# Moving the head of the last layer ahead by one iteration, and weighing two key tiles per run, in a four-layer attention kernel

## The chip, the cores and the metric

One of the eight cores of a Trainium2 chip runs the kernel. The metric is the device time of one execution in microseconds (us), as the median of several runs.

## The reference

The input is a batch of 8 images of 256 channels and 32 x 32 points (1024 tokens each). Four attention layers follow one another; each image passes them alone, so the batches are independent.

```
layer 0: th, ph, g = three 1x1 convolutions to 32 channels; lat = softmax(th^T ph) g^T
         x = x + gamma_sa * conv(lat); then attention to 128 fixed concepts; x = x + gamma_moca * conv(lat2)
layer 1: q, k of 32 channels, v of 256; x = x + gamma * (softmax(q^T k) v)
layer 2: group norm; q, k, v of 256 channels, one head; x = x + proj(softmax(q^T k / 16) v)
layer 3: group norm; 8 heads of 32 channels; softmax attention; output projection wo;
         layer norm over the channels; x = x + the result
```

Every softmax is over 1024 keys for 1024 queries. Everything is in fp32 to the accuracy of the reference; the scores are formed from high and low parts in fp32r.

## The kernel before

**Two lanes.** The work of a batch b is two generators per engine: `front(b)` (layers 0, 1, 2) and `back(b)` (layer 3). Each yields after every small group of instructions. `batches` strings them together: first `front(0)` beside `front(1)`, then for b = 0 to 5 `front(b + 2)` beside `back(b)` (the main loop, six iterations), at last `back(6)` beside `back(7)`. `merged` takes from the one or the other by the table `ORDER`, written out by hand for each stage and engine: lengths of alternate stretches, beginning with the second lane. Within an engine the order is thus fixed, and an instruction that waits holds all behind it. The front lane owns four of the eight PSUM banks, the back lane the other four.

**A softmax layer.** PE forms the scores of one tile of 128 queries against all 1024 keys (`max_tile`, L627: two matmuls into two banks); DVE reduces them to a negated maximum per query (`maximum`, L1285). The maxima are turned into a row and multiplied in with the queries (`shift_rows`: on PE, L634, in the front lane; in the back lane by DVE's transpose and four small transfers of SP, L463). Then PE forms the scores again with keys on the partitions (`stacked_scores`, L641; in layer 2 L837 and L840), ACT takes the exp from PSUM (L1008 in the front, L1138 in the back), and PE weighs the values with them (L697, L755, L918). The sums of the weights come from adds on POOL (L523, L555) and DVE (L1446) and a matmul with ones (L762, L930); ACT inverts them by Ln and Exp (L1017, L1020), DVE multiplies (L1334, L1454).

**The back lane.** Its head: group norm (DVE L1348 and small steps, PE L797 and L801, ACT L1054 to L1060, result in `hb`), queries and keys of the first four heads (PE L608, ACT casts the high parts L1067, DVE the low parts L1280, into `part`), the values (PE L616, copies to `vb` L1025 and L1326). SP then copies `part` into the stacks `qs` and `ks` of the four heads with 24 transfers (L477, 128 KB each). Then two rounds u = 0, 1 of four heads each (`both_rounds`): `maxima(u)`, 4 x 8 tiles; `middle(u)`, in round 0 the queries and keys of the other four heads; `steps(u)`, 16 steps, one for each tile of 128 keys and half of the queries. A step has four score matmuls (one per head) into three banks taken in turn; `score_use` and `total_use` number their uses, `bank_use` tells whose exp frees a bank. The four exps of a step go to `prb`, which holds two steps. `weigh(s - 1)`, issued between the second and third scores of step s, is four matmuls with 32 columns each, side by side in column tiles of the array (L918; eight instructions, as an fp32 matmul is two). Last come the output projection (L608), the layer norm (L958, L1187 to L1206, L1498, L1502) and the store; when a back is through, SP loads the image for its buffer (L488).

**Stages of an iteration in the rows.** A, 754.6 to 863.5 us: the front's layer 0 beside the back's head, its first maxima and the second projections. B, to 953.2: layer 1 beside the first 16 steps. C, to 1007.2: the group norm and projections of layer 2 beside the second maxima. D, to 1119.8: attention of layer 2 beside the second 16 steps, the output projection and the layer norm.

## Time and profile before

| what | value |
|---|---|
| median of 3 runs | 3000.66 us (2998.16 to 3001.39) |
| the profiled execution | 3000.55 us, span 2998.4 us |
| mean granted clock of TensorE | 0.89 |
| PE matmul / weight load busy | 91% / 47% |
| DVE, ACT, POOL busy | 60%, 40%, 30% |
| fronts stage ends, first iteration ends | 392.7 us, 754.6 us |
| the iteration shown below | 754.6 to 1119.8 us, 365.2 us |
| last stage begins | 2577.3 us |

A busy time sums the durations of an engine's instructions without overlap. A matmul at half clock is busy twice as long, so a high busy share does not say that PE is at its peak. "Idle before" gives the time the engine stood before the instruction and what it is inferred to have waited for.

### The profile page before, as it was taken

The numbers are of one execution on the slowest core, as the hardware profiler recorded it, in microseconds if no ns is written. First come the engines' busy times: TensorE is split into PE (matmuls) and PEld (weight loads), VectorE is DVE, ScalarE is ACT, GpSimd is POOL, SyncE is SP. The second block draws the span as 40 slices with busy tenths as digits, with TensorE's granted clock in tenths as the row PEclk, the third lists the DMA queues.
The fourth block names the chain that finished last, engine by engine and source line by source line (L and its number), as shares of the span: only waits on it lengthen the run. The fifth ranks groups of instructions, "written<-read, shape, count | busy, mean of one in ns | idle before, by whom it ended". The sixth has DMA issues, their size and how long they took to land.

```text
span 2998.4 us, 25561 instructions
## 1 busy us (share of the span) xinstructions
PE 2740.4 (91%) x9636; PEld 1415.0 (47%) x9636; DVE 1795.9 (60%) x1749; ACT 1209.4 (40%) x2073; POOL 897.0 (30%) x362
## 2 busy tenths in 40 slices
PE   7999989999899998999889998999989989798887
PEld 4546644455444544445444454444544445443332
DVE  4535057673676647765476654767447583488884
ACT  3332223535344442534426254262532625325455
POOL 0040311614025240333304242061510615115563
PEclk8899988989788998989979898798987989879787
DMA  2000010100201002010010100101020100211100
GB/s 83 1 0 0 1 43 1 43 1 6 65 1 43 1 17 54 1 42 1 28 43 1 42 1 29 42 14 30 1 56 15 40 3 1 64 36 43 43 1 28
DMA packets 29291, 72.08 MB, mean 24 GB/s; under 512 B 10224, under 2 KB 10416, under 8 KB 28912
## 3 DMA queue, kind: packets, MB, share of 16 engines
q1 hardware_dynamic: 29168, 70.45, 9.4%
q8 instruction: 76, 1.25, 0.2%
q14 instruction: 47, 0.39, 0.0%
HBM read 11.40 MB, written 8.39 MB: 7 GB/s over the span
## 4 chain that ended last, share of the span: by engine, by line
PE 71%; DVE 17%; issue 3%; ACT 3%; SPq 2%; DMA 2%; POOL 1%; DVEq 0%; ACTq 0%; POOLq 0%
PE ps L755 13%; PE ps L608 12%; PE ps L641 9%; PE ps L627 9%; PE ps L918 7%; PE ps L840 6%; DVE ba_nmx L1285 5%; PE ps L616 4%; SPq L477 2%; PE ps L697 2%; DVE accb L1446 2%; PE ps L826 2%; DVE fa_nmx L1285 1%; PE ps L930 1%; PE ps L837 1%
## 5 line engine op out<-in xcount | busy, mean ns | idle before, releaser
L1138 ACT ACTIVATE prb<-ps 128x512 f32<-128x512 f32 x896 | 489.1, 598 | 367.7 <-PE ps L641 341.1
L1285 DVE TENSOR_REDUCE ba_nmx<-ps 128x1 f32<-128x1024 f32 x448 | 531.0, 1215 | 77.9 <-PE ps L627 76.2
L555 POOL TENSOR_TENSOR accb<-accb,prb 128x1024 f32<-128x1024 f32 x168 | 440.8, 2624 | 179.0 <-ACT prb L1138 174.8
L627 PE MATMUL ps<-ks,qs 96*128 96x512 f32 x896 | 419.5, 575 | 74.6 <-DVE ba_nmx L1285 69.0
L555 POOL TENSOR_TENSOR accb<-prb 128x1024 f32<-128x1024 f32 x28 | 80.2, 2864 | 1306.8 <-ACT prb L1138 1247.3
L755 PE MATMUL ps<-pr,h 128*128 128x512 f32 x896 | 421.1, 594 | 0.2
L1446 DVE TENSOR_TENSOR accb<-accb,prb 128x1024 f32<-128x1024 f32 x168 | 317.8, 1892 | 155.8 <-ACT prb L1138 154.1
L641 PE MATMUL ps<-qs,ks 97*128 97x512 f32 x896 | 351.6, 464 | 8.6 <-ACT prb L1138 7.5
L627 PEld LDWEIGHTS ps<-ks,qs 96*128 96x128 f32 x896 | 195.3, 248 | 268.6 <-DVE ba_nmx L1285 201.9
L641 PEld LDWEIGHTS ps<-qs,ks 97*128 97x128 f32 x896 | 160.7, 192 | 228.1 <-ACT prb L1138 157.0
L1008 ACT ACTIVATE pr<-ps 128x512 f32<-128x512 f32 x336 | 194.5, 598 | 175.9 <-PE ps L641 112.5
L755 PEld LDWEIGHTS ps<-pr,h 128*128 128x128 f32 x896 | 167.4, 189 | 162.8 <-issue 143.4
L918 PE MATMUL ps<-prb,vb 128*32 128x512 f32 x1792 | 243.4, 616 | 0.7 <-ACT prb L1138 0.7
L1334 DVE TENSOR_TENSOR tmp<-tmp,rden 128x512 f32<-128x512 f32 x56 | 46.7, 866 | 311.9 <-ACT rden L1020 311.9
L1285 DVE TENSOR_REDUCE fa_nmx<-ps 128x1 f32<-128x1024 f32 x168 | 198.9, 1216 | 17.9 <-PE ps L826 12.2
L523 POOL TENSOR_TENSOR acc<-acc,pr 128x1024 f32<-128x1024 f32 x56 | 153.0, 2732 | 138.8 <-ACT pr L1008 138.8
L608 PE MATMUL ps<-hb,w 128*128 128x512 f32 x368 | 175.8, 632 | 2.0 <-ACT hb L1060 2.0
L840 PE MATMUL ps<-q2k 128*128 128x512 f32 x672 | 173.4, 393 | 0.0
L523 POOL TENSOR_TENSOR acc<-pr 128x1024 f32<-128x1024 f32 x28 | 69.1, 2467 | 338.8 <-ACT pr L1008 301.8
L840 PEld LDWEIGHTS ps<-q2k 128*128 128x128 f32 x672 | 126.7, 189 | 36.4 <-issue 10.3
L608 PE MATMUL ps<-h,w 128*128 128x512 f32 x272 | 139.1, 649 | 1.3 <-DVE bb_nmx L1285 1.3
L627 PE MATMUL ps<-ks,q2k 96*128 96x512 f32 x224 | 90.5, 509 | 36.2 <-DVE fa_nmx L1285 24.6
(303 smaller groups left out, 3402.4 us busy)
## 6 DMA issues: line engine op xcount, KB each, us to landing
qs<-part SPq DMA_DIRECT2D x168, 128.0 KB, 2.4
ks<-part SPq DMA_DIRECT2D x168, 128.0 KB, 2.4
xm<-in_x SPq DMA_DIRECT2D x8, 1024.0 KB, 5.6
out<-prb SPq DMA_DIRECT2D x28, 256.0 KB, 2.0
q2k<-part SPq DMA_DIRECT2D x48, 128.0 KB, 2.4
w<-in_weights SPq DMA_DIRECT2D x1, 2592.0 KB, 8.7
out<-pr SPq DMA_DIRECT2D x4, 256.0 KB, 2.0
qs<-ba_nmx_r SPq DMA_DIRECT2D x56, 4.0 KB, 1.8
```

What stands on the lines that cost most here:

```text
L523: pool.tensor_tensor(o.acc[:], before if jg == 1 else o.acc[:], now, ALU.add).then_inc(o.summed[n].sem, 1)
L555: pool.tensor_tensor(o.sums[1], o.pairs[(s - 1) % 2][1] if j == 1 else o.sums[1], o.pairs[s % 2][1], ALU.add)\
L608: mm = pe.matmul(o.ps[0:m, bank, :], wcol(name, kt, m0, m), src[:, kt, cols(ic)], start=kt == 0, stop=kt == CH - 1)
L627: mm = pe.matmul(o.ps[:, bank + jc, :], queries[0:STACK, tile(it)], keys[0:STACK, cols(jc)], start=True, stop=True)
L641: return pe.matmul(o.ps[:, bank, :], keys[0:ROW + 1, tile(jt)], queries[0:ROW + 1, cols(ic)], start=True, stop=True)
L755: mm = pe.matmul(o.ps[:, 2 + ch, :], o.v[:, jt, tile(ch)], o.pr[:, t % 4, :], start=jt == 0, stop=jt == NT - 1)
L840: mm = pe.matmul(o.ps[:, bank, :], kpart[:, kt, keys], qpart[:, kt, cols(ic)], start=False, stop=kt == CH - 1 and kpart is o.kl2)
L918: mm = pe.matmul(o.ps[L * g:L * g + L, 2, :], o.vb[:, jt, L * (QUAD * u + g):L * (QUAD * u + g + 1)], weights3(o, s, g), start=jt == 0, st ...
L1008: act.activation(o.pr[:, t % 4, :], o.ps[:, bank, :], ACT.Exp).then_inc(o.exped[n].sem, 1)
L1138: act.activation(weights3(o, s, g), o.ps[:, turn3[score_use(s, g) % 3], :], ACT.Exp)\
L1285: dve.tensor_reduce(o.nmx[:, head, it:it + 1], o.ps[:, bank:bank + 2, :], AX.XY, ALU.max, negate=True).then_inc(o.max_sb[n].sem, 1)
L1446: dve.tensor_tensor(o.sums[0], o.pairs[(s - 1) % 2][0] if j == 1 else o.sums[0], o.pairs[s % 2][0], ALU.add)\
```

## The change

It does two things. **The head.** `back(b)` now yields the word "head" when its head is issued (on PE after the values, on ACT and DVE after the copies of the values, on SP after the first stacks, on POOL at once). `batches` makes the backs beforehand and appends the head of `back(b + 1)` behind `back(b)` on its lane, beside the front of the same iteration; the head of `back(0)` is appended behind `front(1)`, whose buffers it takes over. The lane then begins the next iteration with the first maxima. **Two tiles of keys.** For batches 0 to 5 (`in_pairs`) PE weighs at even steps only, after the first two scores: `weigh(s - 2)` and `weigh(s - 1)` one behind the other, 16 column-tiled instructions; the last pair follows the last scores. For batches 6 and 7 it stays one per step. The first sum of weights takes its bank two uses later and ACT's inversion moves by two exps, in all batches.

The tables `ORDER` are all new. What stands in them for the main loop, on PE, read off by counting:

| | before | after |
|---|---|---|
| head: norm, q, k, v | among the front's first 13 items | norm after score 13 and 14 of layer 2, q and k after score 15; v behind the front's last item |
| first maxima (32) | 2 before the front's scores of layer 0, 15 more beside these and the weighing, rest to the end of layer 0 | 8 before them, 7 of them beside the 8 front tiles; 9 beside the scores, rest to the end of layer 0 |
| second projections | before the front's last four matmuls of layer 0 | behind them |
| second maxima (32) | 8 before the sum that ends layer 1, 24 behind it | all behind it, the last two beside the first tiles of layer 2's maxima |
| second 16 steps | begin before layer 2's maxima | begin before the last of the 8 tiles |
| output projection | near layer 2's score 14 | near its score 11 |

On DVE the reductions are placed alike: before, 23 back tiles lie between the front's last maximum and its first transpose of layer 0, after the change 14. In the fronts stage the head comes behind the last item of both fronts. In the last stage `back(6)` begins with maxima, beside the head of `back(7)`.

The diff without the tables:

```diff
@@ -147,12 +149,21 @@
         pass
 
 
+def head(last_layer):
+
+    for slot in last_layer:
+        yield
+        if slot == "head":
+            return
+
+
 def batches(engine, front, back):
 
-    finish(merged("fronts", engine, front(0), front(1)))
+    last = [back(b) for b in range(B)]
+    finish(merged("fronts", engine, front(0), chain(front(1), head(last[0]))))
     for b in range(B - 2):
-        finish(merged("both", engine, front(b + 2), back(b)))
-    finish(merged("backs", engine, back(B - 2), back(B - 1)))
+        finish(merged("both", engine, front(b + 2), chain(last[b], head(last[b + 1]))))
+    finish(merged("backs", engine, last[B - 2], last[B - 1]))
 
 
 def both_rounds(maxima, middle, steps):
@@ -392,11 +403,15 @@
         def sq(o, ch, ic):
             return o.pairs[1][ch][:, ic, :]
 
+        def in_pairs(b):
+
+            return b < B - 2
+
         def score_use(s, g):
-            return QUAD * s + g + (s >= NT + 2)
+            return QUAD * s + g + (QUAD * s + g >= total_use(0))
 
         def total_use(ic):
-            return (QUAD * (NT + 2), QUAD * STEPS3 + 1)[ic]
+            return (QUAD * (NT + 2) + 2, QUAD * STEPS3 + 1)[ic]
 
         def bank_use(o, u, use):
 
@@ -481,6 +496,8 @@
                 def back(b):
                     for u in range(CH):
                         yield from stacks(b, u)
+                        if u == 0:
+                            yield "head"
                         yield from shift_rows(b, u)
                     for ic in range(IC):
                         if ic and b + 3 < B:
@@ -541,6 +558,8 @@
                     yield from sums(b, 2)
 
                 def back(b):
+                    yield "head"
+
                     def steps(u):
                         for s in range(STEPS3):
                             ic, j = divmod(s, NT)
@@ -862,7 +881,7 @@
                         done = (o.q_lo, o.k_lo)[half][3]
                         pe.wait_ge(done.sem, done.at(b, IC))
                         values("v3", o.hb, 2 * half, half).then_inc(o.v_ps[3].sem, 1)
-                        yield
+                        yield "head" if half else None
                     for half in range(2):
                         pe.wait_ge(o.v_sb[3][half].sem, o.v_sb[3][half].at(b, 1))
                     def maxima(u):
@@ -931,16 +950,19 @@
                                                start=True, stop=True, tile_position=(0, L * g))
                             mm.then_inc(o.total[3].sem, 1)
 
+                        together = 2 if in_pairs(b) else 1
                         for s in range(STEPS3):
                             yield from scores(s, 0)
-                            if s:
-                                weigh(s - 1)
+                            if s and s % together == 0:
+                                for before in range(s - together, s):
+                                    weigh(before)
+                                yield
+                            if s == NT + 2:
+                                sum_weights(0)
                                 yield
                             yield from scores(s, 1)
-                            if s == NT + 1:
-                                sum_weights(0)
-                                yield
-                        weigh(STEPS3 - 1)
+                        for before in range(STEPS3 - together, STEPS3):
+                            weigh(before)
                         yield
                         sum_weights(1)
                         yield
@@ -1151,7 +1173,7 @@
                     if b == B - 1:
                         act.wait_ge(backs[0].l3_g.sem, backs[0].l3_g.at(B - 3, 4))
                     take_values(b, 3, 0, o.vb, 0)
-                    yield
+                    yield "head"
 
                     def middle(u):
                         if u == 0:
@@ -1165,9 +1187,9 @@
 
                     def steps(u):
                         for s in range(STEPS3):
+                            yield from exps3(u, s, 0)
                             if s == NT + 2:
                                 yield from invert(b, 3, IC * u + 1, turn3[total_use(0) % 3], o.rdenb[:])
-                            yield from exps3(u, s, 0)
                             if s == NT:
                                 take(u, 0)
                                 yield
@@ -1459,7 +1481,7 @@
                     if b == B - 1:
                         dve.wait_ge(backs[0].l3_g.sem, backs[0].l3_g.at(B - 3, 4))
                     take_values(b, 3, 1, o.vb, 2)
-                    yield
+                    yield "head"
 
                     def maxima(u):
                         for k in range(QUAD * NT):
```

## Rows read from the trace of the kernel before

**Rows 1.** The page: busy time of the engines, and the costliest group of exps.
```profile
PE 2740.4 (91%) x9636; PEld 1415.0 (47%) x9636; DVE 1795.9 (60%) x1749; ACT 1209.4 (40%) x2073; POOL 897.0 (30%) x362
...
L1138 ACT ACTIVATE prb<-ps 128x512 f32<-128x512 f32 x896 | 489.1, 598 | 367.7 <-PE ps L641 341.1
```

**Rows 2.** Windows (us and length, then PE, PEld, DVE, ACT, POOL busy, clock, DMA).
```profile
754.60:863.50 108.90, 91.35 (x261) 48.23 (x260) 75.81 (x86) 28.44 (x43) 0.00 (x0) 0.76 0.18 44
863.50:953.20 89.70, 88.64 (x368) 42.62 (x368) 52.98 (x38) 54.52 (x97) 56.70 (x22) 1.00 0.16 36
953.20:1007.20 54.00, 46.72 (x121) 25.89 (x121) 43.64 (x56) 8.57 (x14) 0.00 (x0) 0.75 0.00 1
1007.20:1119.80 112.60, 111.30 (x454) 58.84 (x452) 50.47 (x38) 59.66 (x107) 54.21 (x22) 1.00 0.02 6
...
880.00:905.00 25.00, 24.07 (x129) 10.46 (x127) 23.16 (x18) 19.03 (x35) 17.68 (x6) 1.00 0.00 1
```

**Rows 3.** Timeline of PE in stage A: start, us, what, idle before it.
```profile
761.05 6.50 PE L608 MATMUL ps<-xm,w 128*128 128x512 f32 x8 [6.42 <-DMA xm<-in_x]
...
772.62 2.07 PE L627 MATMUL ps<-ks,q2k 96*128 96x512 f32 x4 [1.80 <-DVE ks L1274]
...
802.81 1.05 PE L641 MATMUL ps<-q2k,ks 97*128 97x512 f32 x2
...
824.77 1.02 PE L713 MATMUL ps<-h,cst 128*64 128x512 f32 x2
...
852.84 7.13 PE L608 MATMUL ps<-hb,w 128*128 128x512 f32 x16
```

**Rows 4.** Timeline of SP's queue, and the chain's step behind it (start, us, what).
```profile
780.23 7.81 SPq L477 DMA_DIRECT2D qs<-part  x12
788.09 7.57 SPq L477 DMA_DIRECT2D ks<-part  x12
...
795.06 2.36 DMA ks<-part
```

**Rows 5.** The chain of waits: start, us, what ran.
```profile
739.80 1.38 PE ps L840 x6
...
1000.67 6.92 PE ps L616 x32
...
1097.84 6.87 PE ps L608 x16
```

**Rows 6.** Timeline of column-tiled runs (L918, L697) and their neighbours.
```profile
909.67 0.40 PE L641 MATMUL ps<-q2k,ks 97*128 97x512 f32 x1
910.00 0.16 PEld L918 LDWEIGHTS ps<-prb,vb 128*32 128x32 f32 x8 [0.37 <-issue]
910.00 1.06 PE L918 MATMUL ps<-prb,vb 128*32 128x512 f32 x8
910.99 0.74 PE L641 MATMUL ps<-qs,ks 97*128 97x512 f32 x2
...
70.98 1.08 PE L697 MATMUL ps<-pr,vgo 128*64 128x512 f32 x4
71.89 1.03 PE L697 MATMUL ps<-prb,vb 128*64 128x512 f32 x4
```

**Rows 7.** Timeline of PE behind the fronts stage's last matmul.
```profile
391.69 1.02 PE L762 MATMUL ps<-accb,ones 128*128 128x512 f32 x2
...
399.70 0.38 PE L797 MATMUL ps<-ba_gn_mv,cst 128*128 128x2 f32 x2 [3.19 <-DVE ba_gn_mv L1353]
400.93 0.38 PE L801 MATMUL ps<-ba_gn_var,cst 128*128 128x2 f32 x2 [0.84 <-DVE ba_gn_var L1366]
...
406.87 9.55 PE L608 MATMUL ps<-hb,w 128*128 128x512 f32 x16
```

**Rows 8.** Timeline of PE at the start of the last stage.
```profile
2576.16 1.10 PE L762 MATMUL ps<-acc,ones 128*128 128x512 f32 x2 [0.41 <-issue]
...
2663.03 2.36 PE L627 MATMUL ps<-ks,qs 96*128 96x512 f32 x4 [0.18 <-DVE ba_nmx L1285]
```

More of the change, by code:

```diff
@@ L22 @@
 from contextlib import ExitStack
+from itertools import chain
 import concourse.bass as bass
@@ L76 @@
     ("fronts", "PE"): (
[19 rows of a table removed]
[19 rows of a table added]
     ("fronts", "ACT"): (
-        0, 4, 4, 14, 1, 2, 1, 2, 1, 1, 9, 1, 3, 1, 5, 4, 5, 12, 2, 2, 4, 1, 2, 1, 1, 2, 1, 2, 2, 3, 8, 3, 2, 1,
-        1, 7, 3, 1, 9, 4, 2, 2, 2, 2, 1, 2, 3, 1, 2, 2, 3, 1, 1, 3, 2, 2, 2, 1, 2, 3, 3,),
+        0, 4, 4, 13, 1, 1, 1, 1, 1, 1, 1, 2, 1, 1, 4, 2, 10, 4, 2, 2, 1, 6, 1, 9, 1, 6, 1, 7, 1, 2, 1, 2, 1, 1,
+        6, 1, 2, 1, 2, 3, 6, 2, 4, 2, 1, 1, 9, 2, 2, 2, 5, 1, 3, 1, 1, 1, 2, 1, 2, 1, 5, 1, 5, 3, 8,),
     ("both", "ACT"): (
-        0, 2, 1, 1, 1, 1, 6, 21, 10, 3, 4, 1, 33, 1, 6, 1, 2, 1, 3, 2, 4, 1, 2, 1, 3, 1, 3, 1, 2, 5, 2, 21, 21,
-        1, 6, 1, 2, 1, 8, 2, 2, 1, 6, 1, 8, 1, 4, 1, 2, 1, 4, 3, 4, 3, 2, 1, 5, 1, 1, 1, 4, 1, 3, 3,),
[3 rows of a table added]
     ("backs", "ACT"): (
-        0, 2, 1, 1, 2, 5, 5, 73, 2, 1, 72, 54, 6, 2, 2, 1, 1, 1, 1, 3, 3, 1, 4, 1, 1, 1, 1, 1, 2, 1, 5, 1, 6, 1,
-        1, 4, 4, 2, 3, 1, 1, 1, 4, 1, 4, 2, 3, 1, 8, 1, 4, 1, 18,),
+        8, 72, 2, 1, 1, 1, 71, 57, 1, 1, 3, 2, 3, 2, 1, 1, 2, 2, 2, 1, 5, 1, 5, 1, 2, 2, 1, 2, 3, 1, 3, 2, 1, 1,
+        2, 1, 3, 1, 4, 2, 6, 1, 9, 1, 26,),
     ("fronts", "DVE"): (
-        0, 4, 1, 2, 1, 2, 1, 2, 1, 2, 8, 8, 1, 1, 1, 1, 1, 2, 2, 4, 1, 1, 1, 1, 1, 2, 4, 3, 11, 11, 1, 1, 2, 5,
-        1, 5, 6, 2, 3, 2, 2, 1, 4, 2, 2, 1, 2, 1, 6, 3, 1, 1, 1, 2, 1, 1, 6, 2, 1, 1, 1, 1, 2, 4, 4,),
+        0, 3, 1, 3, 2, 3, 2, 3, 7, 14, 3, 1, 1, 1, 1, 5, 3, 2, 4, 1, 1, 1, 1, 11, 2, 1, 1, 1, 1, 2, 1, 3, 1, 3,
+        3, 15, 41, 1, 1, 3, 6, 4, 16,),
     ("both", "DVE"): (
[3 rows of a table removed]
[3 rows of a table added]
     ("backs", "DVE"): (
[4 rows of a table removed]
[4 rows of a table added]
     ("fronts", "POOL"): (
-        0, 5, 4, 3, 4, 1, 1, 3, 3, 2, 2, 1, 1, 1, 1,),
+        0, 8, 6, 1, 2, 3, 1, 1, 1, 1, 4, 1, 2, 1, 1,),
     ("both", "POOL"): (
-        10, 1, 3, 1, 1, 6, 6, 1, 3, 1, 3, 2, 2, 4,),
+        7, 1, 1, 1, 1, 1, 2, 1, 1, 1, 2, 3, 7, 1, 2, 1, 5, 1, 1, 5,),
     ("backs", "POOL"): (
-        0, 14, 14, 11, 1, 1, 1, 1, 3, 1, 9,),
+        0, 6, 1, 8, 14, 12, 2, 1, 1, 1, 11,),
     ("fronts", "SP"): (
-        0,),
+        7,),
     ("both", "SP"): (
-        16,),
+        17,),
     ("backs", "SP"): (
-        0, 6, 6, 7, 7, 1, 1, 2, 2,),
+        6, 1, 1, 6, 7, 1, 1, 1, 1, 1, 1,),
 }
```

51 rows, old and new, of the table ORDER are left out of this document.

## The prediction

> **What bounds the kernel now.** The page comes first: TensorE (PE) is busy 91% of the span [rows 1]. That looks like a bound, but it is a mean over stages with different limits, and matmuls at half clock count as busy. So the second view is one iteration of the main loop cut at the points where the PE stream changes stage, 754.6 to 1119.8 us [rows 2]. The reader should see two kinds of stage. In B (863.5 to 953.2) and D (1007.2 to 1119.8) PE is busy 99% at granted clock 1.00: these are bound by PE. In A (754.6 to 863.5) and C (953.2 to 1007.2) it is busy 84 and 87% at clock 0.76 and 0.75, which is a mixture of the two levels, 2.4 and 1.2 GHz; VectorE (DVE) is busy 75.8 of 108.9 us and 43.6 of 54.0 us. There the time is set by dependencies and by DVE's reductions, 1.27 us per tile of maxima with the handshake (two in 2.36 + 0.18) [rows 8], and PE stretches its work to fill. The third view, PE's timeline, shows why A is long [rows 3]: both lanes begin with latency. PE stands 6.4 us until the next image has come, runs eight projections at the low clock in 6.5 us, waits 5 us for the casts, and reaches the first scores only at 802.8. The back lane's first maxima wait for the stacks: SP issues 24 transfers one behind the other, 7.8 and 7.6 us, and the last lands 2.4 us later [rows 4].
>
> **Sum, iteration by iteration.** I compare the profiled execution (3000.55 us, span 2998.4; the median of the runs is 3000.66, the same within 0.01%). At full clock 16 projection matmuls take 6.87 us, the 32 of the values 6.92 us, and a plain score or maxima matmul 1.38 / 6 = 0.23 us [rows 5]. (A matmul in fp32 counts as two instructions in the rows.)
>
> *A, the head moved.* Without the change: wait 6.4, projections 6.5, casts 5.1, then 30.2 to the first scores (the head's 48 matmuls are in it), 22.0 of scores, 38.7 to the end, the four projections of the second half (7.1) included [rows 3]. With it: the values of the head are the last that PE runs, after the front's last matmul, 6.9; they hide the front's normalisation and the image has been loaded, since the back ended earlier. Projections at full clock 3.4 (half of 6.87) and casts 4.4 (5.1 less what the head's casts mixed in, an estimate). By the new order 7 back tiles and 8 front tiles then alternate, 15 x 1.27 = 19. The front's row of maxima 3. Scores: before, 17 back reductions lay beside them (22.0 = 17 x 1.29, so DVE set that), now some 12, 15. The rest was 38.7 with 15 back tiles, is 31.6 without the four projections and 29 with 13 tiles; the projections 6.9 to 7.1. Sum 6.9 + 3.4 + 4.4 + 19 + 3 + 15 + 29 + 7.1 = 87.8, **21.1 us less**.
>
> *The stacks.* SP starts the first transfers when the queries are cast, about 9 us before PE's last front matmul (two key projections 3.4; 14 matmuls of weighing and summing at 0.43, 6). 15.4 + 2.4 later is 8 to 10 us past it; PE first asks after 6.9 + 3.4 + the transposes, about 12. Covered by a few us; if the front's tail were shorter, this would be the wait. SP's outputs of the old back stand ahead of them in its queue, but these end before the head's normalisation starts.
>
> *B.* Two tiles in one run of column-tiled matmuls. One run of 8 takes 0.99 us to the next start, plus 0.10 at entry (909.67 to 910.00 is 0.33 where a plain matmul takes 0.23) and 0.11 at exit (the two matmuls behind it end 0.34 apart, 0.74 - 0.40): 1.20. Where one column-tiled run follows another, 70.98 to 71.89, the first takes 0.91 [rows 6], near the bare 0.86 of two fp32 passes at 0.43 [rows 5] with the tiles side by side. A pair so costs about 2.1 in place of 2.4, 0.31 saved; the bounds are 0 (the halves don't flow) and 0.34 (all overhead of one run). Eight pairs per round: 2.5 us. Eight back maxima, 16 matmuls x 0.23 = 3.7, leave B for C. Against it, ScalarE (ACT): the first exp of the even step waits until the first half of the pair is over, while before that half had run a step earlier. PE can start the run when the third exp of the odd step is out, ACT has one exp (0.60) [rows 1] left and the half run takes 1.0 plus a score 0.24: ACT stands about 0.7. It matters where ACT is the pace, in 880 to 905 it is busy 19.0 of 25 us [rows 2] and next to the first four pairs the front has no exps: 4 x 0.7 = 2.8. Elsewhere the front's matmuls cover it. B: -2.5 - 3.7 + 2.8 = **3.4 us less**.
>
> *C.* The new order starts the second round's maxima after the front's layer 1, not beside its end. 8 back tiles more and 2 of the front: 10 x 1.27 = 12.7; six front tiles more then lie between the back's maxima and its steps, 7.6. DVE was idle 10.4 us in C and takes part of that up, I take 6.8, two thirds, since the wait for the front's last normalisation now stands open. 12.7 + 7.6 - 6.8: **13.5 us more**, between 9.9 (all idle taken up) and 20.3 (none).
>
> *D.* It loses the matmuls of eight front maxima (32 x 0.23 = 7.4) and the pairs' 2.5. It gains the head's projections 6.9, the norm's small matmuls 0.5 and two stalls, as PE takes its instructions in order: for the group norm's statistics and for its scale, 3.4 together, an estimate: the two chains take 7.0 us (392.7 to 399.7) and 5.6 us (401.3 to 406.9) [rows 7], and the new order puts one to three layer-2 steps of about 3.3 us (seven matmuls of 0.23, four of 0.43) between them. **0.9 us more.**
>
> One iteration: -21.1 - 3.4 + 13.5 + 0.9 = -10.1. Six of them: **-61**.
>
> **The two ends.** In the fronts stage the head stands bare, behind both fronts' last matmul. By [rows 7] it is 7.0 us from there to the first norm matmul and 7.2 on to the projections, of which the front's own matmuls put between are 2; these take 6.9 at full clock and 13.7 at half, I take 10, as the first idle drops the clock: 7.0 + 5.2 + 10 = **+22**, between 19 and 26. In the last stage both heads used to start together: 2577.3 to 2665.4, 88.1 us to the last of 32 reductions [rows 8]. Now the stacks land at 10, 32 x 1.27 = 40.6 and DVE's part of batch 7's head, 9.2 (four statistics, four casts, one copy of values and the small steps, an estimate from A's 10 us of the same), make 59.8, **-28**. Total -61 + 22 - 28 = -67: 3000.6 - 67 = **2933**.
>
> **A rule against the pairs.** In the trace the 8 weight loads of a run, about 109 ns each, cover 0.16 us together and start with the run [rows 6]: column tiles load side by side and beside running matmuls. The Trainium skill ("TensorE: Matmul & The Clock Gate", Part 3, The mechanism) says that weight loads overlap matmuls in flight only when their row group differs; column tiles share it. By that rule the second half's loads would wait for the first half and a pair would save nothing; the trace speaks against it for one run, but no run of 16 is shown.
>
> **Rivals.** (1) *More gain*: A and C run at DVE's pace. A's DVE work is 75.8, less some 10 of the head, 66; plus 11 before it can start, 77: 11 us more per iteration, total -67 - 66: **2867**. For: the new order leaves no 5 us hole for DVE in A. Against: before, DVE idled 33 us in A beside a full queue. Chance 0.2. (2) *The pairs don't flow*: each costs two runs, 96 x 0.31 = 30 lost: **2963**. Chance 0.1. (3) *Slower, ACT held at every pair*: if ACT stands a whole run (1.06) at each of 96 pairs and PE, which has three banks for scores, stands behind it, 102 us go, of which 17 are counted: -67 + 85 = +18, **3018**. It decides from (67 + 17) / 96 = 0.87 us per pair. For: ACT is three quarters busy there. Against: PE has 66 us of other matmuls in B and more in D to run meanwhile. Chance 0.09. (4) *Nothing*: C's 20 us and a late stack (4) eat A's gain, -21 - 3 + 20 + 4 = 0 per iteration, and the ends give 22 - 28 = -6: **2995**, chance 0.06.
>
> **Numbers.** The forecast has 0.55. 0.2% (6 us) is about what can be told from no change here. Faster: 0.55 + 0.2 + 0.1 + a little of the rest = 0.86; same 0.05; slower 0.09. Range: up to 2985 leaves out the last two rivals; down to 2865 takes in the first; C's bounds alone (-3.6 to +6.8 per iteration, times six) give 2911 to 2974, A's (scores still 22 us, or 11 us quicker as in rival 1) 2975 and 2867.
>
> **What would show it.** Right: an iteration of about 355 us; PE goes from a front's last summing matmul to the head's values without the 6.4 us gap; first scores about 38 us later; stage C longer, about 67 us; runs of 16 column-tiled matmuls in about 1.9 us; the last stage some 28 us shorter; the first stage 22 us longer. Wrong: a wait for the stacks at the start of A; idle before the first maxima; ACT idle near 1 us before each pair's exps; a second half of a pair that takes as long as the first with its drain; an iteration over 362 us.

## The result and the profile after

The changed kernel takes 2979.52 us (median of 4, 2974.67 to 2981.09), the kernel before in the same comparison 2999.64: ratio 0.993, 95% interval 0.9913 to 0.9947. That is 20 us less; 67 were forecast. The profiled execution took 2980.27 us, span 2978.2, mean granted clock 0.891 (before 0.89).

The page of the changed kernel first, the busy times, beside [rows 1]. PE is busy the same 91% of the span and DVE has the same work; no work was dropped.

```profile
PE 2715.4 (91%) x9636; PEld 1438.7 (48%) x9636; DVE 1796.2 (60%) x1749; ACT 1199.1 (40%) x2073; POOL 904.3 (30%) x362
...
L1160 ACT ACTIVATE prb<-ps 128x512 f32<-128x512 f32 x896 | 487.1, 603 | 358.5 <-PE ps L660 189.5
```

Then the windows of the second iteration of the main loop, cut where [rows 2] cut it: A, B, C, D (us and length, busy PE, PEld, DVE, ACT, POOL, clock, DMA).

```profile
776.40:877.36 100.96, 89.28 (x249) 46.66 (x248) 68.62 (x68) 22.54 (x33) 0.00 (x0) 0.75 0.07 17
...
877.36:962.34 84.98, 82.51 (x349) 40.45 (x348) 50.72 (x32) 52.18 (x95) 59.11 (x22) 0.98 0.14 32
962.34:1028.74 66.40, 56.54 (x161) 34.06 (x161) 57.31 (x68) 10.43 (x16) 0.00 (x0) 0.79 0.04 9
1028.74:1138.34 109.60, 108.55 (x446) 58.67 (x445) 47.50 (x50) 64.08 (x116) 54.56 (x22) 1.00 0.12 34
```

| stage | before | forecast of the difference | measured difference |
|---|---|---|---|
| A | 108.9 | -21.1 | -7.9 |
| B | 89.7 | -3.4 | -4.7 |
| C | 54.0 | +13.5 | +12.4 |
| D | 112.6 | +0.9 | -3.0 |

Three stages came within 4 us; A missed by 13. Over the run (with the ends of the fronts' last sums as marks): the fronts stage +4.4, the first iteration +17.4, the other five together -13.4, the last stage -28.6 (421.1 to 392.6). So the last stage gave its 28, and the loop almost nothing. The iterations are not quite alike: the five behind the first take 359.1 to 364.3 us (before 362.2 to 365.2), and their A 99.5 to 101.4.

PE's timeline in A shows what held and what did not (start, us, line, idle before it). It answers to [rows 3].

```profile
776.24 7.07 PE L635 MATMUL ps<-w,hb 128*128 128x256 f32 x32
783.15 3.60 PE L627 MATMUL ps<-xm,w 128*128 128x512 f32 x8
789.11 0.68 PE L690 MATMUL ps<-cst,pr 32*128 32x32 f32 x8 [2.36 <-DVE pr L1409]
...
810.56 1.05 PE L660 MATMUL ps<-q2k,ks 97*128 97x512 f32 x2
...
832.18 1.93 PE L732 MATMUL ps<-h,cst 128*64 128x512 f32 x4
...
856.64 7.19 PE L756 MATMUL ps<-acc,wo_con 64*128 64x512 f32 x8 [0.18 <-DVE acc L1332]
863.76 1.22 PE L646 MATMUL ps<-ks,qs 96*128 96x512 f32 x2
864.78 3.62 PE L627 MATMUL ps<-xm,w 128*128 128x512 f32 x4
868.19 7.57 PE L627 MATMUL ps<-hb,w 128*128 128x512 f32 x16
875.59 1.88 PE L627 MATMUL ps<-xm,w 128*128 128x512 f32 x4
877.36 0.71 PE L660 MATMUL ps<-qs,ks 97*128 97x512 f32 x2
```

The start of A is what was forecast: the head's values begin 0.16 us before the mark, fill the 6.4 us hole, and the image's projections follow at once at full clock. The first scores come 34.2 us after the mark (forecast 36.7). From there on it is late. The scores take 21.6 us (810.56 to 832.18) in place of 15, and the tail of the stage, the `wo` projections (L756), a projection of layer 1, the second half's q and k and another of layer 1, takes 20.7 us. The four instructions at 864.78 take 3.62 us, four of the same form at 875.59 take 1.88: the first ran at 1.2 GHz, the second at 2.4. In C, PE waits for the second round's stacks behind SP's queue; PE's timeline, then SP's:

```profile
961.22 1.12 PE L781 MATMUL ps<-acc,ones 128*128 128x512 f32 x2 [0.51 <-POOL acc L545]
965.44 2.08 PE L646 MATMUL ps<-ks,qs 96*128 96x512 f32 x4 [3.09 <-DMA ks<-part]
```

```profile
948.50 7.51 SPq L492 DMA_DIRECT2D qs<-part  x12
956.05 7.58 SPq L492 DMA_DIRECT2D ks<-part  x12
```

### The profile page after: what moved, and what is told of

Read it like the earlier page. It is cut to its first block, busy times and chain, and to the rows that moved or that the text cites. A ratio compares the mean times of both kernels' runs of the same rounds, so it can differ in the third digit from the quotient of the medians.

```text
span 2978.2 us, 25567 instructions
## 1 busy us (share of the span) xinstructions
PE 2715.4 (91%) x9636; PEld 1438.7 (48%) x9636; DVE 1796.2 (60%) x1749; ACT 1199.1 (40%) x2073; POOL 904.3 (30%) x362
## 4 chain that ended last, share of the span: by engine, by line
PE 65%; DVE 24%; ACT 4%; issue 3%; POOL 1%; SPq 1%; DVEq 1%; DMA 0%; ACTq 0%; POOLq 0%
PE ps L627 12%; PE ps L774 11%; PE ps L660 8%; PE ps L646 7%; DVE ba_nmx L1307 6%; PE ps L937 6%; PE ps L859 5%; PE ps L635 5%; DVE fa_nmx L1307 4%; DVE accb L1468 3%; PE ps L716 2%; PE ps L756 2%; PE ps L845 2%; DVE tmp L1356 1%; DVE prb L1520 1%
## 5 line engine op out<-in xcount | busy, mean ns | idle before, releaser
L574 POOL TENSOR_TENSOR accb<-accb,prb 128x1024 f32<-128x1024 f32 x168 | 458.5, 2729 | 125.7 <-ACT prb L1160 117.6
L646 PE MATMUL ps<-ks,qs 96*128 96x512 f32 x896 | 401.0, 559 | 98.7 <-DVE ba_nmx L1307 71.1
L937 PE MATMUL ps<-prb,vb 128*32 128x512 f32 x1792 | 226.6, 617 | 0.7 <-ACT prb L1160 0.7
L540 POOL TENSOR_TENSOR acc<-acc,pr 128x1024 f32<-128x1024 f32 x56 | 142.8, 2551 | 108.7 <-ACT pr L1030 107.5
L627 PE MATMUL ps<-hb,w 128*128 128x512 f32 x368 | 167.1, 608 | 3.1 <-ACT hb L1082 2.4
L1089 ACT ACTIVATE part<-ps,vec 128x512 fp32r<-128x512 f32 x64 | 43.9, 687 | 220.4 <-PE ps L627 206.1
L1468 DVE TENSOR_TENSOR accb<-prb 128x1024 f32<-128x1024 f32 x28 | 34.2, 1223 | 137.6 <-PE ps L949 130.5
```

What stands on the lines that cost most here:

```text
L540: pool.tensor_tensor(o.acc[:], before if jg == 1 else o.acc[:], now, ALU.add).then_inc(o.summed[n].sem, 1)
L574: pool.tensor_tensor(o.sums[1], o.pairs[(s - 1) % 2][1] if j == 1 else o.sums[1], o.pairs[s % 2][1], ALU.add)\
L627: mm = pe.matmul(o.ps[0:m, bank, :], wcol(name, kt, m0, m), src[:, kt, cols(ic)], start=kt == 0, stop=kt == CH - 1)
L646: mm = pe.matmul(o.ps[:, bank + jc, :], queries[0:STACK, tile(it)], keys[0:STACK, cols(jc)], start=True, stop=True)
L937: mm = pe.matmul(o.ps[L * g:L * g + L, 2, :], o.vb[:, jt, L * (QUAD * u + g):L * (QUAD * u + g + 1)], weights3(o, s, g), start=jt == 0, st ...
L1468: dve.tensor_tensor(o.sums[0], o.pairs[(s - 1) % 2][0] if j == 1 else o.sums[0], o.pairs[s % 2][0], ALU.add)\
```

## The experiments

All times are medians. A run's number says how it stands to the kernel before, run on the same chip beside it.

**The two halves apart.** Two kernels: the new order with single tiles, and the old order with pairs.

```diff
 # e1_head_only, against the changed kernel
+                            if s:
+                                weigh(s - 1)
                             if s and s % together == 0:
-                                for before in range(s - together, s):
-                                    weigh(before)
...
 # e2_pairs_only, against the kernel before
-                                weigh(s - 1)
+                                if b >= B - 2:
+                                    weigh(s - 1)
+                                elif s % 2 == 0:
+                                    weigh(s - 2)
+                                    weigh(s - 1)
```

> The changed kernel with the pairs undone: PE weighs one tile of keys per step again, at the same place as in the kernel before; head and order tables as changed. Theory H (the pairs save about 0.31 us each on PE, and that counts where PE is full, 96 x 0.31 = 30 us, less what ACT stands for them): this run is 15 to 30 us longer than the changed kernel's 2979.5, about 3000, so that the head and the new tables alone give almost nothing. Rival R (ACT stands for the pairs about as long as PE saves): within 8 us of 2979.5; the head alone brought the whole gain of 20 us.

> The kernel before with nothing but the pairs for batches 0 to 5, in its old order tables. Theory H: stages B and D are full on PE, 16 pairs an iteration save up to 5 us each iteration, less ACT's stand beside the front's maxima (0.7 us for some eight pairs): an iteration 0 to 5 us shorter, the kernel at 2970 to 3000. Rival R: the old tables were laid for one tile per step, so ACT stands for a run at most pairs and the kernel is slower, 3005 to 3030.

Head alone: 3001.76 us, ratio 1.0007 (0.9997 to 1.0018), nothing; theory H said about 3000. Pairs alone: 2969.43 us, ratio 0.9903 (0.9888 to 0.9918), at the lower end of theory H and 10 us better than both together. So the order of the work, which carried nearly all of the forecast, gained nothing. Where the profiled executions spend their time:

| us | fronts stage | first iteration | other five | last stage |
|---|---|---|---|---|
| before | 392.7 | 361.9 | 1822.6 | 421.1 |
| pairs alone | 388.5 | 360.3 | 1809.3 | 409.1 |
| head alone | 395.4 | 387.0 | 1825.9 | 391.5 |
| changed (both) | 397.1 | 379.3 | 1809.2 | 392.6 |

With the head alone the second iteration is 365.0 us long: A 98.7, B 84.7, C 66.5, D 115.1. C gives back 12.5 of the 15.1 that A and B gain, and D 2.5; the last stage's gain of 29.6 us goes, but for 5, on the bare first head. The pairs alone run the same instructions as before in the fronts stage and in the last one (pairs are for batches 0 to 5 only), and yet 16 of their 31 us lie there; the six iterations give 15. So half of what the run with pairs alone gained is not a saving of the pairs but a shift of the low clock, as the last section shows, and the 10 us by which it beats the changed kernel lean on it.

The pairs pay 22 us in the new order (3001.8 to 2979.5), 24 in the loop of the profiled executions. From the windows of D one sees where (head alone; the changed kernel's D stands above):

```profile
1032.28:1147.35 115.07, 111.99 (x446) 57.52 (x445) 49.05 (x50) 64.67 (x116) 54.66 (x22) 1.00 0.12 33
```

PE's busy time is 3.4 us longer than with pairs (8 pairs at 0.31 make 2.5), and it stands 3.1 us where it stood 1.05. The groups by line say what that idle time is, and what a run costs (head alone, then the changed kernel: busy, mean ns of one, idle before):

```profile
L937 PE MATMUL ps<-prb,vb 128*32 128x512 f32 x1792 | 241.4, 611 | 14.7 <-ACT prb L1159 14.7
```

```profile
L937 PE MATMUL ps<-prb,vb 128*32 128x512 f32 x1792 | 226.6, 617 | 0.7 <-ACT prb L1160 0.7
```

In the new order a single run waited for the exp that it weighs, 14.7 us in all; a pair asks only every other step and waits 0.7. I had put a wait of ACT on the pairs' bill; they saved one of PE. D so gets 5.5 us shorter. A gets 2.3 us longer (98.7 to 101.0), all of it in its scores, from the row of maxima to L732: 25.2 us at clock 0.78 for 22.8 at 0.88. Why the clock is lower there with pairs, no run shows.

That a run of 16 flows is plain in the timeline of the changed kernel. It is 1.86 us to the next start; with 0.10 and 0.11 for entry and exit that makes 2.07 where two runs took 2.40 by [rows 6], 0.33 saved for the 0.31 of the sum. The weight loads of the second half run beside the matmuls, so the rule that the prediction set against the pairs does not hold here:

```profile
889.33 1.92 PE L937 MATMUL ps<-prb,vb 128*32 128x512 f32 x16
889.79 0.13 PEld L937 LDWEIGHTS ps<-prb,vb 128*32 128x32 f32 x4 [0.30 <-issue]
890.22 0.13 PEld L937 LDWEIGHTS ps<-prb,vb 128*32 128x32 f32 x4 [0.30 <-issue]
891.19 0.73 PE L646 MATMUL ps<-ks,q2k 96*128 96x512 f32 x2
```

**What sets the scores.** I had read the old phase as 17 reductions at 1.29 us, DVE's pace. The next kernel moves the 9 back tiles out from between the front's scores and issues them behind the last weighing (PE's table of the order alone).

```diff
 # e3_scores_bare: PE's order in the main loop, layer 0
-score 0, 1, max 8, score 2, max 9, score 3, weigh 0, max 10, ..., max 16, weigh 6, 7, max 17, 18, latents
+score 0, 1, 2, 3, weigh 0, score 4, 5, weigh 1, ..., weigh 7, max 8, 9, ..., 18, latents
```

> The changed kernel with one edit in PE's table of the main loop: the nine back tiles of maxima that lie among the front's scores of layer 0 come behind them. Theory V (my prediction's: DVE's reductions set the length of that stretch): from first score to the matmuls behind the last weighing it takes 12 to 15 us in place of 21.6, the maxima behind add 9 x 1.27 = 11.4, stage A changes by -3 to +5. Theory P (the stretch is set by the chain score, exp, weighing in PE's order, and by the low clock that the waits bring): it stays at 17 to 21 us, and the nine tiles behind come on top: an iteration is 7 to 11 us longer, the kernel 35 to 65 us longer than 2979.5.

3048.99 us, ratio 1.0168 (1.0129 to 1.0206), 69 us more than the changed kernel, beyond the 35 to 65 of theory P; an iteration is 10.1 us longer, where it said 7 to 11. The timeline of the bare phase:

```profile
819.31 1.05 PE L654 MATMUL ps<-q2k,ks 97*128 97x512 f32 x2
...
829.13 1.08 PE L710 MATMUL ps<-pr,vgo 128*64 128x512 f32 x4
830.14 0.73 PE L654 MATMUL ps<-q2k,ks 97*128 97x512 f32 x2
830.80 1.08 PE L710 MATMUL ps<-pr,vgo 128*64 128x512 f32 x4
...
836.17 1.21 PE L640 MATMUL ps<-ks,qs 96*128 96x512 f32 x4
...
849.26 1.11 PE L726 MATMUL ps<-h,cst 128*64 128x512 f32 x1
```

With no tile of maxima between them the scores still take 16.9 us (819.31 to 836.17): two scores and a weighing come every 1.67 us (829.13 to 830.80), 8 such steps are 13.4, the rest is the half clock at the start. So PE sets this phase, and each tile of maxima between the scores adds two matmuls of 0.23. In the changed kernel 11 tiles lie there: 16.9 + 11 x 0.46 = 22.0, measured 21.6. Before, PE ran 14 (not the 17 of my count; DVE made 16 reductions in that time): between 13.4 + 14 x 0.46 = 19.8 and 16.9 + 6.4 = 23.3 us, measured 22.0, as near as DVE's 17 x 1.29. Two explanations fitted one number; I had taken the wrong one. A window of the kernel before over just this phase would have told them apart, PE busy all of it and DVE 17.2 of 22.0 us:

```profile
802.81:824.77 21.96, 21.96 (x77) 10.16 (x76) 17.24 (x16) 9.61 (x17) 0.00 (x0) 0.89 0.00 1
```

Laid bare, the 11 tiles in front of the latents then wait for DVE one by one (836.17 to 849.26, 13.1 us), and the run pays it.

**The clock, by more work.** A has PE at 0.75 of the full clock. If that costs, extra PE work that keeps the clock up must make the kernel faster. The next kernels repeat the maxima's matmuls of some tiles of the first back round, into the same place with the same values, in iterations 0 to 5. A tile has two such matmuls, one instruction each; doubled it has four in all (the second expectation below says four for the two).

```diff
 # e4_maxima_twice; the later ones differ in the condition
-                    for jc in range(IC):
-                        mm = pe.matmul(o.ps[:, bank + jc, :], queries[0:STACK, tile(it)], keys[0:STACK, cols(jc)],
+                    for jc in range(2 * IC if n == 3 and b < B - 2 and count < QUAD * NT else IC):
+                        mm = pe.matmul(o.ps[:, bank + jc % IC, :], queries[0:STACK, tile(it)], keys[0:STACK, cols(jc % IC)],
 # e5_twice_outside: (count < 8 or 16 < count < QUAD * NT)
 # e9_twice_late:    (16 < count < QUAD * NT)
 # e10_twice_early:  (count < 8)
```

> The changed kernel, but the two score matmuls of every back tile of maxima in the first round are issued twice (the same values into the same banks), for batches 0 to 5: PE gets 64 matmuls more per iteration, 14.7 us at full clock, mostly in stage A where it waits. Theory K (A is slow because its waits drop the granted clock to 0.75, and the work between them is on the path): the clock in A rises above 0.9, A gets shorter by 2 to 8 us in spite of the added work. Rival L (the chain of latencies and DVE set A, the clock matters little): the clock rises but A stays within 2 us or gets longer by up to 8 us; the kernel is between 2979 and 3030.

> Left as in the changed kernel, but for each tile of keys of the first back round whose maxima don't lie beside the front's latent scores (23 of the 32, in six of the eight iterations), PE issues the four matmuls of the maxima twice, the second time into the same place with the same values; the result is the same. With all 32 tiles doubled the run took 2962.8 us against 2979.5 of the changed kernel, its mean granted clock 0.929 against 0.891, and the scores phase had grown from 25.2 to 30.0 us with nine more groups of matmuls in it. Theory 1 (PE's own work sets the scores phase, and its granted clock the rest of the stage): the phase is back at 25 us or less, the stage from the end of the front's sum to the back's first step at about 95 us, the iteration at about 355 and the run at 2935 to 2960 us. Rival (the doubled matmuls beside the scores are what holds the clock up, or the phase is set by DVE): the stage stays at 100 us and the run at 2963 us or above.

All 32 twice: 2962.81 us, ratio 0.9876 (0.9858 to 0.9893), 17 us faster than the changed kernel with more instructions; the scores phase (from the rows of maxima to L732) grew from 25.2 to 30.0 us, since it is PE's. Neither theory had this. A's clock rose to 0.92, but A stayed at 100.4 us, as rival L said, since the end of the stage gained the 5 us that the scores lost; the run gained in B (83.5 for 85.0) and C (65.0 for 66.4) and came out below L's 2979. Without the 9 tiles of that phase: 2940.76 us, ratio 0.9807 (0.9792 to 0.9822). Its stage A is 95.6 us and its iteration 355.0 (770.55 to 1125.53); 95 and 355 were expected.

> The changed kernel with the maxima's matmuls twice only for tiles 17 to 31 of the first back round, those behind the front's latent scores. With tiles 0 to 7 doubled too it took 2940.8 us, its stage from the front's sum to the back's first step 95.6 us against 101.0. Theory 1 (what costs is the low clock under the wo projections, the q1k1 run and xm at the end of the stage; the stretch of low clock ahead of the rows of maxima hides behind DVE): the end of the stage is 15.4 us as with both, the stage 96 and the run within 5 us of 2940.8. Rival (the early doubled matmuls carry a part, by keeping the clock up into the scores): 2950 to 2970 us, the scores phase longer than 25.2.

> The changed kernel with the maxima's matmuls twice only for tiles 0 to 7, those ahead of the front's latent scores. Theory 1 (the end of the stage is what costs): the end of the stage stays at 20 us or more, the clock rises only in the stretch ahead of the rows of maxima, and the run stays within 6 us of the changed kernel's 2979.5. Rival (a low stretch avoided early moves or spares the later ones): 2940 to 2965 us, the end of the stage 15 to 17 us.

Late tiles alone: **2936.04 us**, ratio 0.9790 (0.9771 to 0.9809), no different from both within the intervals. Early alone: 2967.83 us, ratio 0.9891 (0.9869 to 0.9912). The first theory holds for the late tiles; for the early ones it put the run within 6 us of 2979.5, and 12 were gained, so the rival had a part of it: the end of the stage took 19.5 us (20.7 in the changed kernel), A 99.4 (101.0) and B 83.5 (85.0). The two gains, 43 and 12, don't add: both together gave 39. The windows of A in four parts, up to the rows of maxima, the scores, the latents, the tail; the changed kernel and then the late tiles doubled:

```profile
776.40:806.98 30.58, 25.19 (x77) 14.79 (x75) 22.86 (x24) 6.49 (x8) 0.00 (x0) 0.73 0.24 54
806.98:832.18 25.20, 25.20 (x82) 12.66 (x82) 14.62 (x13) 11.22 (x19) 0.00 (x0) 0.78 0.00 1
832.18:856.64 24.46, 18.18 (x58) 10.81 (x57) 21.52 (x21) 2.08 (x2) 0.00 (x0) 0.77 0.00 0
856.64:877.36 20.72, 20.72 (x34) 8.40 (x35) 9.62 (x13) 2.75 (x4) 0.00 (x0) 0.70 0.01 1
```

```profile
770.37:800.94 30.57, 25.15 (x76) 14.82 (x75) 22.86 (x24) 6.47 (x8) 0.00 (x0) 0.75 0.24 54
800.94:825.89 24.95, 24.95 (x86) 12.94 (x86) 15.08 (x13) 11.22 (x19) 0.00 (x0) 0.83 0.00 1
825.89:851.71 25.82, 24.14 (x81) 15.56 (x81) 21.23 (x21) 2.08 (x2) 0.00 (x0) 0.80 0.00 1
851.71:867.08 15.37, 15.29 (x37) 6.61 (x37) 9.44 (x13) 2.75 (x4) 0.00 (x0) 1.00 0.01 1
```

The first part lasts 30.6 us whatever the clock (with all early tiles doubled it was 0.94), in each of these iterations of every kernel with the new order; DVE, busy 22.9 of it, and the casts are what is left to set it. The latents' part is 18.2 us of matmuls in 24.5, with DVE busy 21.5, and the work put there costs 1.4 us. The tail is PE's alone, busy 20.72 of 20.72, so the clock's level is its time: 20.72 at 0.70, 15.37 at 1.00. In the five iterations behind the first the tail takes 15.4 us in every kernel with the late tiles doubled, and 19.4 to 21.0 in every other kernel of the new order. So what the clock does in the tail follows from how loosely PE was fed in the part ahead. Three of the tail's entries in the timeline with the late tiles doubled, which took 7.19, 3.62 and 7.57 us in the changed kernel:

```profile
851.71 3.70 PE L756 MATMUL ps<-acc,wo_con 64*128 64x512 f32 x8
...
856.61 1.99 PE L627 MATMUL ps<-xm,w 128*128 128x512 f32 x4
858.43 7.03 PE L627 MATMUL ps<-hb,w 128*128 128x512 f32 x16
```

In the changed kernel no gap of PE between 810 and 864 is longer than 1.7 us, and the clock fell all the same. The Trainium skill ("TensorE: Matmul & The Clock Gate", section A second HAM failure mode: psum-queue depth-cycling) says that frequent short gaps between groups of matmuls made the clock swing in one kernel, where its other case is one of long waits for DMA. The trace agrees: in the latents' part no gap is longer than 1.7 us, PE is busy 18.18 of 24.46 us, and the granted clock is 0.77.

**Where it does not help.** The same trick in the old order with pairs, for 16 tiles of the first round, and for 19 tiles of the second round besides.

```diff
 # e6_pairs_twice, on e2_pairs_only
+ (count < 2 or 17 < count < QUAD * NT)
 # e8_pairs_twice_both
+ (... or QUAD * NT + 4 < count < QUAD * NT + 24)
```

> The kernel before with the pairs alone (its order of the work, the last layer's head after the front's sum; that took 2969.4 us), and the matmuls of the maxima issued twice for the first back round's tiles 0, 1 and 18 to 31 (16 of 32, six iterations). Theory 1 (the low clock of the stage ahead of the back's first step is what costs, in either order of the work): the clock rises from 0.90 to above 0.915 and the run takes 2945 to 2965 us, less than any kernel so far. Rival (in this order PE has no room, so that the doubled matmuls lengthen the stage by their own 16 times 0.2 to 0.4 us in each of six iterations): 2970 to 3000 us.

> As the run before last (pairs alone in the order of the kernel before, maxima twice for 16 tiles of the first round), and also twice for tiles 5 to 23 of the second round, which lie in the stage between the first round's end and the second's first step. Theory 1 (that stage is bound by DVE and the stacks, so that PE's clock there doesn't matter): no more than 3 us from the run with 16 tiles doubled, though its mean clock is higher by 0.01 or more. Rival (the low clock of that stage costs too, as in the first): 5 to 20 us less than it. Third: the doubled matmuls come onto the path, 5 to 20 us more.

The first: 2998.94 us, ratio 1.0004 (0.9985 to 1.0022), 30 us slower than the pairs alone, as the rival's 2970 to 3000 had it. Of the 33 us between the two profiled executions 20 lie in the loop, the rest in the fronts and last stages, where nothing was edited. In the loop A carries it, but unevenly: 0.9 and 1.1 us shorter in the first two iterations, 3.0 to 7.1 longer in the others. The fourth, pairs alone and then with the doubled tiles, and the second with them (107.44 us at 0.81 without):

```profile
1472.77:1579.94 107.17, 88.41 (x261) 47.22 (x261) 75.69 (x86) 28.40 (x43) 0.00 (x0) 0.81 0.18 45
```

```profile
1478.11:1592.38 114.27, 97.97 (x292) 55.35 (x293) 76.23 (x86) 28.40 (x43) 0.00 (x0) 0.81 0.17 42
...
750.92:857.24 106.32, 89.56 (x292) 49.76 (x293) 75.97 (x86) 28.40 (x43) 0.00 (x0) 0.89 0.18 45
```

In the fourth the added matmuls are there (PE's busy time +9.6) and the clock is the same 0.81. In the first two it rose to 0.89 and the stage came out shorter, as theory 1 had it; in the others it is 0.81 to 0.85. So it is not only that PE has no room: the added work costs where it fails to raise the clock, and why it fails in four of six iterations is open. The tail of A is 3.6 us long there, at full clock already, with nothing to win, and the long projections stand among the latents.

The second kernel answers for C: 3004.86 us, ratio 1.0014 (0.9997 to 1.0030), 6 us from the first, with intervals that overlap. Its C took 53.45 us at clock 0.90 (PE busy 49.2), that of the pairs alone 53.18 at 0.78 (PE busy 45.6). In that order C does not hear PE's clock.

**Pairs in one round only.**

```diff
 # e7_pairs_second_round, in the changed kernel
+                            if s and u == 0 and together == 2:
+                                weigh(s - 1)
                             if s and s % together == 0:
-                                for before in range(s - together, s):
-                                    weigh(before)
+                                if not (u == 0 and together == 2):
+                                    for before in range(s - together, s):
+                                        weigh(before)
```

> The changed kernel with the pairs only in the back's second round; in its first round PE weighs one tile of keys behind each step, as before. Theory 1 (the first round's stage is set by DVE and ScalarE, and the pairs pay in the second round's stage alone): within 5 us of the changed kernel's 2979.5 us, with the stage of the first round at 85 us as in it. Rival (each round gives half of what the pairs give, some 22 us against the same order of the work with single tiles): about 2990 us, and the stage of the first round 1 to 2 us longer.

2977.32 us, ratio 0.9952 (0.9924 to 0.9979), the changed kernel's time. Its D is 109.6 us. Its B is 84.7 us in the first two iterations and 86.0 in the other four, at clock 0.98; the changed kernel's is between 83.5 and 86.4, in sum 5 us less. Its A is 98.4 to 99.5 us behind the first iteration, in sum 8 us less than with pairs in both rounds. So the pairs of the first round save a little in B and lose it again in A; in the run they pay nothing.

**Is the clock's gain the pairs' own?** The late tiles doubled in the new order with single tiles (e11), and in the seventh iteration too (e12).

```diff
 # e11_head_late: e1_head_only with (16 < count < QUAD * NT)
 # e12_late_last: e9_twice_late with
-n == 3 and b < B - 2 and
+n == 3 and b < B - 1 and
```

> The new order of the work with single tiles instead of pairs (that took 3001.8 us, no less than the kernel before), and the maxima's matmuls twice for tiles 17 to 31 of the first back round, as in the run that took 2936.0. Theory 1 (moving the head gains 10 us in each iteration's first stage and gives them back in the stage of the second round's stacks, and only with PE's clock held up at the end of the first stage does something stay; pairs and clock act in different stages, so they add): about 43 us less than 3001.8, 2950 to 2968 us. Rival (the doubled matmuls pay only together with the pairs): 2985 us or more.

> The run with tiles 17 to 31 doubled (2936.0 us), and the same in the seventh iteration too, in the stage in which the last two backs run together. Theory 1 (there PE waits for DVE's maxima, and some of the low clock of the last stage goes): 2928 to 2935 us. Rival (the doubled matmuls fall among the last latents' projections and steps, and lengthen that stage by their own 3 to 6 us, or change nothing): 2936 to 2942 us.

e11: 2979.76 us, ratio 0.9928 (0.9912 to 0.9945), between the theory's 2968 and the rival's 2985; neither held. Doubling is worth 22 us there and 43 with the pairs; equally, the pairs are worth 22 us without it and 44 with it. The windows of B and C in the kernel with pairs and late tiles doubled show why:

```profile
867.08:950.61 83.53, 81.11 (x349) 39.98 (x348) 50.65 (x32) 52.19 (x95) 59.07 (x22) 1.00 0.14 32
950.61:1015.82 65.21, 55.31 (x161) 32.90 (x161) 57.22 (x68) 10.43 (x16) 0.00 (x0) 0.82 0.04 9
```

A falls by 4.3 us with single tiles and with pairs (98.7 to 94.4, 101.0 to 96.7). But in B the changed kernel had lost the pairs' gain to a short fall of the clock (0.98, 84.98 us); at 1.00 it is 83.53, 1.2 us below the 84.7 of single tiles. C is 1.2 us shorter, 65.2 against 66.4. So doubling is worth 4.3 + 1.5 + 1.2 = 7.0 us in each of six iterations with pairs (42), and 4.3 less 0.7 (C went from 66.5 to 67.2, B stayed 84.7) with single tiles (22). What sets B's clock and C's change is not settled: B fell to 0.98 in two of e11's iterations and in four of e7's as well, which weigh single tiles in that round, and e5, with B at 83.5, has C at 66.3. e12: 2939.81 us, ratio 0.9805 (0.9790 to 0.9819), nothing gained in the last stage (393.8 us against 390.2, of the profiled executions), as the rival had it. In medians of the runs:

| | single tiles | pairs |
|---|---|---|
| order of before | 2998.9 (the kernel before) | 2969.4 |
| new order | 3001.8 | 2979.5 |
| new order, late tiles twice | 2979.8 | 2936.0 |

## Why the prediction came out as it did

The direction was right and the size wrong: 2979.5 lies in the range (2865 to 2985), 46 us above the forecast. The ends came to what was forecast (-5.5 for -6); the whole miss is in the six iterations, -15 us for -61. By the steps of the second iteration:

*A* is the step that failed: 87.8 us forecast, 101.0 measured, 13.2 us too little. Three parts make it up. (1) "22.0 = 17 x 1.29, so DVE set that, now some 12, 15": it stayed 21.6, +6.6. DVE did not set it: e3 shows that PE's own scores and weighings do, and with the clock at 0.94 (e5) it still takes 20.4 (805.92 to 826.32). The range had this as its bound ("scores still 22 us", 2975). (2) The end of the stage was costed at full clock, the second half's projections at 7.1 and the `wo` projections within the 29 of the latents. The clock stood at 0.70 there, 20.7 us instead of 15.4, +5.3, most of it in the `wo` projections (7.2 for 3.7) and the first of layer 1's (3.6 for 2.0). e4, e5 and e9 show it, all three with a tail of 15.4. (3) The sum left out layer 1's own projections, which the new order puts in front of the back's first step, two times 1.8 us at full clock: +3.6. Against these stands the start, 2.5 better (34.2 for 36.7); 6.6 + 5.3 + 3.6 - 2.5 = 13.0 of the 13.2.

*The stacks* of round 0 were covered in the steady iterations, as said (the transposes' wait of 2.36 us is for DVE). In the first iteration PE waited for them, 1.67 us.

*B*: -4.7 for -3.4, but not by the sum's terms. The order alone gives it all (84.7), since layer 1's projections, 3.6 us, left it for A and the sum had missed that too. And 5 tiles of the second maxima left it, not 8: the trace of the kernel before has 10 of their matmuls ahead of the mark at 953.2, 2.3 us. The pairs gain 1.2 only where the clock stays at 1.00.

*C*: +12.4 for +13.5, near by luck. The sum moved 16 reductions into C; DVE ran 12 more (68 instructions for 56 in the windows), 5 of the back and 7 of the front, 13.7 us of work for 20.3. And it let them take up 6.8 us of DVE's idle time, where 1.3 went (10.4 to 9.1), with 3.1 us of waiting for the second stacks that I had not named. The two errors cancel.

*D*: -3.0 for +0.9. The head costs it 2.5 (e1; 3.4 by my terms with the pairs taken out), the pairs give 5.5, twice the 2.5 that I gave them, since PE's wait for the exps went too.

*The ends*: the last stage -28.6 for -28. A part of it can be chance: in e2 the same instructions as before took 409.1 us in that stage, not 421.1. The bare first head: A of the first iteration is 119.7 us against 101.0 in the next, 18.7, and the fronts stage ahead of it, newly ordered too, takes 4.4 us more, 23.1 together where 22 were forecast. That the ends fit rests on this sum of two, one of which was not in it.

*The rivals.* None came as such. What (4) said of a late stack and C's cost was near the mark (the new order alone: nothing), with the loss in another place. (3), ACT held, didn't happen. (2) is excluded: a run of 16 flows. (1), A at DVE's pace, is excluded by e9: with the clock up A is 96.7 us, of which DVE works 68.6.

*What would show it*: "an iteration over 362 us" was the sign of a wrong prediction, and 361.9 stood just below it.

## What to carry to other kernels

Where PE sets a stage alone, count it at the clock that the part ahead of it leaves, not at full clock: here a partly fed stretch (PE busy 18.2 of 24.5 us) was paid in the dense run behind it, 20.7 us for 15.4. If such a stretch waits for another engine anyway, matmuls repeated into the same place can be nearly free and buy the clock back (43 us here), but look for a dense tail behind it first; in another order like work cost 30 us. And when a phase's time fits "17 of one engine's instructions", work out the other engine's own sum before choosing: both fitted here, and only one of them still held after the change. A window over just that phase, with both busy times, decides it before anything is built. At last, compare a change stage by stage: of the 31 us that the pairs alone seemed to bring, 16 lay in stages that they do not touch.

## What was not expected of the hardware

More PE work made the kernel faster: the two matmuls of 15 tiles issued again, 30 instructions more in each of six iterations, 2979.5 to 2936.0 us. The clock can fall with no gap of PE longer than 1.7 us in the stretch ahead of it. And the last stage, with the same instructions in the same order, took 421.1 us in the kernel before and 409.1 in e2, at mean clock 0.81 and 0.85 (PE busy 350.1 and 336.9 us); the fronts stage, unchanged as well, took 392.7 and 388.5. So a change elsewhere shifts where the low stretches fall, by up to 12 us, which is more than several of the effects that I had summed. What carries the shift from one stage into the other, no run here shows.
